# First-level steps of a four-layer graph network, each placed at its own distance from the block, in place of one group per block

## What is computed

```
x = layernorm(x + L0(x))   # MLP 64-128-64, then a sum over edges with weights 1/sqrt(deg deg), + self
x = layernorm(x + L1(x))   # the same kind, with edge weights, between its two linear steps too
x = layernorm(x + L2(x))   # attention over the edges of a target
x = layernorm(x + L3(x))   # an MLP on each edge, summed by target, then an MLP on each node
```

## Time and profile before

| | us |
|---|---|
| median of 3 runs | 2968.99 |
| the three runs | 2963.08 to 2969.27 |
| the profiled execution | 2964.16 |
| its span | 2962.4 |

### The profile page before, as it was taken

One profiled execution on the slowest core, in us unless ns is written; L12 is line 12 of the kernel. 1 busy time (PEld: TensorE's weight loads), 2 busy tenths in 40 slices (PEclk: granted clock), 3 DMA queues, 4 the chain that ended last, 5 costly groups with the idle time before them and its releaser, 6 DMA issues.

```text
span 2962.4 us, 39045 instructions
## 1 busy us (share of the span) xinstructions
PE 2167.5 (73%) x10332; PEld 1145.4 (39%) x10332; DVE 1987.5 (67%) x3848; ACT 1436.1 (48%) x2755; POOL 2174.0 (73%) x1666
## 2 busy tenths in 40 slices
PE   3998999959878646766577768998355576666665
PEld 1444444434444323434344434444255333333332
DVE  5665688858888747788599985777599433333332
ACT  2876677746545335565345446676222232233232
POOL 7888877778887258888588858888333688888887
PEclk9999999979989868897799979999655687777777
DMA  7998522223666366767354443443387322222221
GB/s 212 277 280 232 140 58 59 56 55 82 138 136 133 93 132 153 164 150 164 84 115 115 114 100 84 99 109 80 80 189 187 84 57 55 56 56 57 56 50 25
DMA packets 624034, 338.13 MB, mean 114 GB/s; under 512 B 536607, under 2 KB 585101, under 8 KB 623818
## 3 DMA queue, kind: packets, MB, share of 16 engines
q1 hardware_dynamic: 550217, 288.96, 38.8%
q0 software_dynamic: 73600, 46.68, 9.3%
HBM read 203.61 MB, written 130.80 MB: 113 GB/s over the span
## 4 chain that ended last, share of the span: by engine, by line
POOL 54%; issue 20%; DVE 11%; PE 9%; DMA 3%; SPq 2%; ACT 1%; DVEq 0%; POOLq 0%; ACTq 0%
POOL g_row L860 38%; POOL x_with_info L867 8%; POOL out_rows L867 7%; PE bank L1078 2%; PE bank L1101 2%; DVE rT L1696 1%; PE pair L987 1%; DMA g_row<-t_x,gidx 1%; DVE agg L1718 1%; PE bank L987 1%; PE pair L1058 1%; DVE x_r L1673 1%; DVE agg L1776 1%; DVE ss L1619 1%; PE pair L1069 1%
## 5 line engine op out<-in xcount | busy, mean ns | idle before, releaser
L860 POOL DMA_INDIRECT g_row<-t_x,gidx x600 | 814.0, 1357 | 263.6 <-issue 218.9
L1288 ACT ACTIVATE hid<-pair,b_up 128x1000 f32<-128x1000 f32 x375 | 406.1, 1083 | 45.9 <-PE pair L1059 44.2
L1079 PE MATMUL bank<-hid,w_dn 128*64 128x500 f32 x750 | 423.6, 648 | 0.0
L1078 PE MATMUL bank<-hid,w_dn 128*64 128x500 f32 x750 | 423.6, 648 | 0.0
L860 POOL DMA_INDIRECT g_row<-x_with_info,src_i x200 | 275.4, 1377 | 69.3 <-issue 56.7
L1058 PE MATMUL pair<-xT,w_top 64*128 64x500 f32 x550 | 314.6, 653 | 13.0 <-ACT hid L1288 10.5
L860 POOL DMA_INDIRECT g_row<-t_h,gidx x200 | 260.4, 1302 | 81.1 <-issue 80.8
L1059 PE MATMUL pair<-xT,w_bot 64*128 64x500 f32 x550 | 315.0, 654 | 0.0
L860 POOL DMA_INDIRECT g_row<-in_x,dst_i x200 | 260.2, 1301 | 68.0 <-issue 67.6
L1269 ACT ACTIVATE xT<-bank 128x500 f32<-128x500 f32 x275 | 160.3, 583 | 280.2 <-DVE rT L1696 163.2
L867 POOL DMA_INDIRECT out_rows<-n_r,fidx x200 | 251.2, 1256 | 60.9 <-issue 60.6
(11 more groups left out here) (257 smaller groups left out, 5157.9 us busy)
## 6 DMA issues: line engine op xcount, KB each, us to landing
x_in<-in_x_cols SPq DMA_DIRECT2D x100, 250.0 KB, 3.2
x_with_info<-wide SPq DMA_DIRECT2D x50, 476.0 KB
wide<-in_x SPq DMA_DIRECT2D x50, 448.0 KB
out_rows<-x_r SPq DMA_DIRECT2D x100, 224.0 KB
l_k<-keep_row SPq DMA_DIRECT2D x150, 125.0 KB
l_a<-t_x SPq DMA_DIRECT2D x150, 112.0 KB
l_k<-on_row SPq DMA_DIRECT2D x50, 250.0 KB
t_x<-x_r SPq DMA_DIRECT2D x100, 112.0 KB
```

The costliest lines, as they stand in the source:

```text
L860: return g.indirect_dma_start(out=to, out_offset=None, in_=table, in_offset=bass.IndirectOffsetOnAxis(ap=index[:, tile:tile + 1], axis=0), ...
L1078: T.matmul(run.down[0:D, 0:CH], w_dn[a.stage][:, 0:D], hid[a.b2][:, 0, :], start=True, stop=True)
L1079: T.matmul(run.down[D:128, 0:CH], w_dn[a.stage][:, 0:D], hid[a.b2][:, 1, :], start=True, stop=True)\
L1288: A.activation(hid[a.b2][:, :, :], run.up[a.b2][:, :, 0:CH], ACT.Relu, bias=b_up[:, a.stage:a.stage + 1]).then_inc(Cn["hid"], 1)
```

## The change

Each first-level step is now tied to its own block's place by a number of slots: a step stands in slot n if some iso block has its place at n minus that number. SP: loads 5, stores 7. PE: aggT 3, after the chain's part of the slot. ACT: root 5, square 4. DVE, between `first` and `rest` as before and in the same order of steps: rstd 6, t1 4, ssum 5, rows 6, t2 4, scans 2. Waits, buffers and instructions are the same; loads of block b+4 are now asked for by block b.

```diff
-        def blocks_due(n):
-            return [a.b for a in ISO if a.place[0] + 2 == n] + [NI + i for i in range(5) if ISO[-1].place[0] + 3 + i == n]
-        def behind(b, lag):
-            b -= lag
-            return (b, b % 2, b % 4) if 0 <= b < NI else None
+        def block_at(n, slots):
+            found = [a.b for a in ISO if a.place[0] + slots == n]
+            return (found[0], found[0] % 2, found[0] % 4) if found else None
...
-            def slot_a(b):
-                if 4 <= b < NI:
-                    ld_a(b)
-                if c := behind(b, 5):
-                    st_a(c[0])
             with_a = sp_chain(WITH_A)
             for n in SLOTS_A:
-                for b in blocks_due(n):
-                    slot_a(b)
+                if c := block_at(n, 5):
+                    if c[0] + 4 < NI:
+                        ld_a(c[0] + 4)
+                if c := block_at(n, 7):
+                    st_a(c[0])
                 with_a(n)
...
-            def slot_a(b):
-                if c := behind(b, 1):
+            with_a = chain(WITH_A)
+            for n in SLOTS_A:
+                with_a(n)
+                if c := block_at(n, 3):
                     k, p, q = c
                     at_least(pe, LA["agg"], 2 * k + 2)
                     at_least(pe, LA["t1"], k)
...
-                if c := behind(b, 3):
+                if c := block_at(n, 5):
                     at_least(act, LA["ssum"], k + 1)
...
-                if c := behind(b, 2):
+                if c := block_at(n, 4):
                     at_least(act, LA["t2"], k + 1)
...
-            def slot_a(b):
-                if c := behind(b, 4):
+            def slot_a(n):
+                if c := block_at(n, 6):
...
-                if c := behind(b, 2):
+                if c := block_at(n, 4):
...
-                if c := behind(b, 3):
+                if c := block_at(n, 5):
...
-                if c := behind(b, 4):
+                if c := block_at(n, 6):
...
-                if c := behind(b, 2):
+                if c := block_at(n, 4):
...
-                if c := behind(b, 0):
+                if c := block_at(n, 2):
...
             for n in SLOTS_A:
                 first(n)
-                for b in blocks_due(n):
-                    slot_a(b)
+                slot_a(n)
                 rest(n)
```

More of the change, by code:

```diff
@@ L1114, in slot_a @@
                     mm.then_inc(LA["aggT"].sem, 1)
-            with_a = chain(WITH_A)
-            for n in SLOTS_A:
-                with_a(n)
-                for b in blocks_due(n):
-                    slot_a(b)
             pe.wait_ge(Cn["rows"], normed_before(WITH_A.hi))
@@ L1327, in slot_a @@
                     A.activation(a_sq[:, :], a_w[p][:, :], ACT.Square).then_inc(LA["sq"].sem, 1)
[L1329 to L1333, removed]
             HB, OB = bank[3], pair[1][:, 1, :]
```

## The result

| | us |
|---|---|
| before, in the comparison of the prediction | 2967.56 (2958.52 to 2977.41) |
| changed, median of 10 runs | 2948.26 (2943.03 to 2955.91) |
| ratio | 0.9937, 95% interval 0.9921 to 0.9953 |
| the profiled execution of the changed kernel | 2943.46, its span 2941.6 |

The change makes the kernel faster by 0.5 to 0.8%. Two more comparisons of the same pair gave 0.9923 (0.9910 to 0.9935) and 0.9957 (0.9944 to 0.9970), so by the ratios the gain is somewhere from 13 to 23 us; the stage itself gained some 14, as follows.

What follows compares the result with a forecast made beforehand. POOL's chain waits for the first level, paced by gathers, then DVE, then SP's loop. Gains of 17.7 in the middle and 3.1 at the end, less 4.6 for SP's queue, give 16.2 us: 2951 us, range 2940 to 2968.

Steps and rivals of the forecast that it cites:

- SP's price: Loads and stores moved ahead of eight stores make DVE's h2 wait, mainly slots 191 and 211: 4.6 us lost.
- the nine bursts: DVE bursts from 187 to 221 lose only ssum, which moves into waits of light slots: 4.6 us gained.
- the queue hides it: Rival, chance 0.13: on SP the eight stores land before DVE asks; gain 20.8 us, time 2946.
- The bound: First level: gathers pace until 763 us, DVE to 1022, then SP's loop; POOL's next gather near 1046 instead of 1062.
- First piece: Up to slot 184: extra DVE work of 5.2 us mostly covered by PE's gather wait; taken as nothing, bound 1.6.
- Split bursts: Five DVE bursts lose rstd, ssum and rows (7.6 us); four lose t1, ssum and t2 (7.5): 15.1 us gained.
- Slots 189, 190, 209 and 210: Split-off DVE work lands in slots 189 and 209, which have no wait: 1.0 us each, 2.0 us lost.
- PE and ACT: aggT leaves the burst without making t1 wait, PE is ready for shorter bursts, ACT is off the path: no cost.
- the slower rival: Chance 0.12: SP's queue delays DVE in nine bursts by 27 us, PE's lower clock adds 9: 2979 us.
- Gathers: POOL's gathers as pace of the middle: argued against, since by 922.69 they run as far ahead as buffers allow.
- The tail: From slot 228 on: less DVE work, an earlier store and a burst without ssum; SP's loop unchanged: 3.1 us gained.
- From the sum to the median: 16.2 us passed on whole to the end: 2948 for the profiled execution, median placed slightly higher at 2951.

Runs made afterwards that it cites:

- the ssum experiment: Changed kernel with ssum and its root back at 6 slots, rstd and rows at 8, row stores at 9, for blocks 0 to 22: 2961.27 us, ratio 0.9976.

## Why the prediction was right, and where its steps were not

The forecast of 2951 us and its direction hold, and the stage gained 14.5 us where the sum said 16.2. But the sum came close because errors cancelled: SP's price was some 5 us too low, the gain of the nine bursts nearly 2 too low, and the smaller terms together another 2 too low; 1.7 us are left of it. The time alone, 2948.26, does not tell the forecast from the rival "the queue hides it" (2946); the waits do. That the medians gained 19 us where 18 were forecast is in part luck: the level gave some 14, and the rest is not explained (the last paragraph of this section).

**The bound.** Right: DVE paces the middle, SP the tail, POOL's next gather marks the end of both. It came at 1049.69, not near 1046: 2 us of that is a later start of the level, 637.51 for 635.54, and 1.7 the smaller gain. DVE's waits for `sd` and PE fell to 13.3 us, not to about 10.

**First piece.** Taken at nothing, measured -0.6. Right.

**Nine bursts without ssum.** The forecast was -4.6, measured -6.3 to -6.5. The mechanism is right (the ssum experiment), the size off. A burst lost 0.82, not 0.60: the 0.81 us from rows to t2 was read as a step's cost, though 0.22 of it was a wait. The Trainium skill (VectorE: DVE Perf Modes, "The DRAIN you can't avoid") says of a chain of eight DVE copies that a semaphore after each costs nothing extra. Here, where an operation waits on the one just ahead, the rows show a price: 0.81 or 0.82 with that wait, 0.60 without.

**Split bursts.** -7.6 and -7.5 forecast; -6.8 and -7.4 measured. In the five, t2 now stands right behind t1, on which it waits: 0.72 from one to the other where t1 took 0.55. Slots 203 and 223 were free, as said. Slots 189, 190, 209 and 210 cost 1.4 instead of 2.0: their slots grew by 1.8, the slots behind shrank by 1.1, since the waits for `sd` and PE in each of them fell from 2.1 to 0.4 while ssum came in: PE's bound there was mostly waiting that now falls under rstd to t2.

**PE and ACT.** Right. In the middle t1 never waits for aggT, and PE no longer waits for t1 (6.3 us in ten times before, shows one).

**SP.** This is the step that was mis-sized: +4.6 forecast, about +10 measured (8.2 with fewer gathers). The mechanism and two of the places are as said; slot 189 is a third. Timeline of SP behind t2 of slot 189, which ends at 793.46:

```profile
793.50 0.87 SPq L666 DMA_DIRECT2D l_src<-l_base  x2
794.41 1.09 SPq L668 DMA_DIRECT2D l_k<-keep_row  x2
795.55 2.23 SPq L673 DMA_DIRECT2D t_x<-n_r  x2
797.82 1.89 SPq L647 DMA_DIRECT2D t_h<-h_r  x4
799.75 1.89 SPq L650 DMA_DIRECT2D t_x<-x_r  x4
```

and of DVE in slots 189 to 192:

```profile
790.18 0.69 DVE L1612 TENSOR_TENSOR h_r<-pair,x_r 125x512 f32<-125x512 f32 x1 [1.39 <-DMA t_x<-x_r]
...
792.78 0.68 DVE L1752 TENSOR_TENSOR l_a<-u_r,l_src 125x512 f32<-125x512 f32 x1
...
803.19 0.69 DVE L1612 TENSOR_TENSOR h_r<-pair,x_r 125x512 f32<-125x512 f32 x1 [4.11 <-DMA t_x<-x_r]
...
811.01 0.20 DVE L1632 RECIPROCAL rs<-sd 125x8 f32<-125x8 f32 x1 [0.70 <-ACT sd L1249]
```

From t2 to h2 it is 9.7 us, not 8.2: `L673` took 2.23 where its row had 1.16, and the landing ended 1.55 after the last issue instead of 1.08. DVE was at h2 after 5.6 us, as said (about 6). So slot 191 waited 4.11 instead of 2.2, slot 211 3.41 instead of 2.2, slot 189 1.39 instead of 0.2: 4.3 us more. The long `L673` belongs to this execution: in the other two profiles of the changed kernel it took 1.1 at this place, but the eight issues behind it took 5.9 and 5.0 instead of 3.8, t2 to h2 came to 11.0 and 10.0, and h2's waits in the middle to 9.7 and 7.7. What stretches an issue wasn't tried. SP's idle time ahead of `L666` and `L673`, 42.4 and 42.0 us from 700 to 1060, is put down to DVE's t2 and rows, as the text had it.

The rest was left out of the sum, though the text priced it in the slower rival: a DVE that waits leaves PE idle. Timeline of PE behind the wait of slot 191:

```profile
809.69 1.22 PE L980 MATMUL pair<-ident,rT 128*125 128x128 f32 x4 [6.27 <-DVE rT L1681]
810.84 1.10 PE L1071 MATMUL bank<-hid,w_dn 128*64 128x500 f32 x1
```

and its window there (length, busy PE, PE clock, DMA share, GB/s):

```profile
809.50:812.00 2.50, 2.31 (x8) 0.50 0.46 106
```

The four matmuls take 1.22 instead of 0.70 and the down products 1.10 instead of 0.63, at a granted clock of 0.50, the lower of the two levels (1.2 GHz), and slots 192 and 212 grew by 0.97 each. The stage's clock fell to 0.88 from 0.90, which the prediction had named as a sign of being wrong: it is one here, of this term.

The rival "the queue hides it" falls: eight issues here took 3.82 us and the landing behind them 1.55, and asking one slot later removed the wait. By the Trainium skill's sentence that the time to initiate a DMA is usually small relative to the DMA itself (DMA: Bandwidth & Descriptors, "Issuing engines are not separate DMA queues") it would have held. One issue of some 0.48 us is about a third of that landing, and in one queue eight of them stand one behind another, so the rule doesn't price this case.

**Gathers.** The text dismissed them, since POOL was ahead by 922.69. For the changed kernel that is right, 0.6 us of waiting. For the rival without the queue it isn't: with the loads later the level gained 17.9 us (426.7 less 408.8) of that rival's 20.8, because the gathers come next. Slots 185 to 228 take 244.9 us with all of them and 236.6 with fewer.

**The tail.** -3.1 forecast, -3.6 measured, and its loop is confirmed.

**From the sum to the median.** The rest beyond the level was taken as unchanged. The medians gained 19, 21 and 14 us in the three comparisons, the level 13.8 on average. The first profiled execution of before had 1895.1 us behind the level, and the changed one 1886.9, the lowest of all; so the 20.8 us between these two executions are 14.5 in the level, less 2 for the later start, and 8.2 behind the level, where the six executions lie from 1886.9 to 1897.3. An effect of the change on the later levels isn't shown.

## What to carry to other kernels

A step that is moved on the compute engines drags its transfers to another place of an in-order queue: list what is issued behind them, and who waits for its landing; one slot later for the loads and stores cost nothing and took all of h2's 8.9 us of waits away, though 4 us of it reached the time while the gathers came next. An idle second engine belongs into the sum of every new wait, not into the pessimist's case alone. And ask what comes next when a bound is lifted: here DVE, SP's queue and the gathers lay within 10 us of 250, while three column loads that waited at the head of the queue in the tail were worth 18.8.

## What the hardware showed that was not expected

- A DVE operation on 125x512 float32 that waits on the one just ahead starts 0.81 us after it, and 0.60 us without that wait; the list of waits shows neither.
- The two issues of the same store (`L673`, 224 and 26 KB) took between 0.87 and 2.23 us of SP's queue.
- 200 gathers of the same shape took 1.27 us mostly, and up to 2.2; their sum differed by up to 3.8 us between executions of one kernel (271.7 to 275.5 in three of before).
